# The expert stage of a gated cross-attention block written out tile by tile, with other distances between its steps

## What is computed

```python
# _L1_ffn_ref, x: [16, 256, 256], E = 8 experts, K = 2 per token, HID = 512
probs = jax.nn.softmax(logits, axis=-1)
_, top_k_idx = jax.lax.top_k(logits, K)
...
gate0 = jnp.einsum('bld,ehd->bleh', x, gating_w[:, 0])
gate1 = jnp.einsum('bld,ehd->bleh', x, gating_w[:, 1])
act = jax.nn.gelu(gate0) * gate1
out = jnp.einsum('bleh,ehd,ble->bld', act, linear_w, combine)
...
x = x + jnp.tanh(g_ffn[1]) * _L1_ffn_ref(_layernorm(x, axis=-1), ...)
```

## Time and profile before

| | us |
|---|---|
| median of 3 runs | 1779.32 (1778.08 to 1781.38) |
| the profiled execution | 1782.04 |
| its span, first to last instruction | 1780.2 |
| PE busy | 1522.6 (86%) |
| DVE busy | 1202.0 (68%) |
| ACT busy | 925.8 (52%) |
| POOL busy | 592.0 (33%) |

### The profile page before, as it was taken

The page is one execution under the profiler, slowest core; times in us unless marked ns, Lnnn a source line. Parts: engine busy times, 40 slices in busy tenths (PEclk is TensorE's granted clock), DMA queues, the critical chain, the costliest instruction groups (busy, mean ns, idle before and its releaser), DMA issues. The chain is left out here.

```text
span 1780.2 us, 36819 instructions
## 1 busy us (share of the span) xinstructions
PE 1522.6 (86%) x12540; PEld 1084.8 (61%) x12541; DVE 1202.0 (68%) x3316; ACT 925.8 (52%) x2530; POOL 592.0 (33%) x777
## 2 busy tenths in 40 slices
PE   3899999999999999999999999986538887888784
PEld 2667676676766767667676776755425454555452
DVE  5478888788887888878888788886433433333332
ACT  4377676766767667676676766755112222222221
POOL 3002323233332333323333233332423444444442
PEclk9899999999999999999999999998759999999997
DMA  7101202021020210202102021031016222222224
GB/s 241 60 1 61 66 7 72 7 67 65 9 72 7 66 61 12 72 7 67 56 18 72 2 71 49 8 109 63 20 58 177 45 44 44 44 44 44 44 44 121
DMA packets 78142, 97.97 MB, mean 55 GB/s; under 512 B 20576, under 2 KB 61680, under 8 KB 77936
## 3 DMA queue, kind: packets, MB, share of 16 engines
q1 hardware_dynamic: 51152, 77.01, 13.6%
q0 software_dynamic: 15872, 18.95, 6.6%
q10 hardware_dynamic: 10976, 0.13, 0.3%
HBM read 65.02 MB, written 35.23 MB: 56 GB/s over the span
## 5 line engine op out<-in xcount | busy, mean ns | idle before, releaser
L801 ACT ACTIVATE prob<-S,nm 128x256 f32<-128x256 f32 x512 | 235.5, 474 | 81.8 <-issue 41.2
L794 ACT ACTIVATE pTh<-T 128x512 f16<-128x512 f32 x256 | 139.5, 597 | 136.0 <-PE T L975 135.8
L1303 PE MATMUL S<-GL,xgh 128*128 x576 | 173.8, 384 | 10.1 <-issue 8.8
L1494 DVE TENSOR_REDUCE mx<-S 128x2 f32<-128x512 f32 x256 | 163.3, 679 | 21.2 <-PE S L1048 20.7
L645 POOL TENSOR_SCALAR ve_ln<-mv_ln 128x2 f32<-128x2 f32 x64 | 14.7, 229 | 470.6 <-DVE mv_ln L1468 469.7
L1506 DVE SCALAR_TENSOR_TENSOR pTl<-T,pTh 128x512 f16<-128x512 f32 x256 | 164.1, 682 | 6.5 <-ACT pTh L794 6.5
L716 POOL DMA_INDIRECT xg<-x_rows,trow x72 | 70.4, 978 | 230.2 <-DMA acc_rows<-ysb,yid 99.3
L810 ACT ACTIVATE prob<-prob,rden 128x256 f32<-128x256 f32 x256 | 116.5, 504 | 56.5 <-DVE p0n L1515 55.8
L975 PE MATMUL T<-ident,prob 128*128 128x128 f32 x1024 | 142.2, 283 | 1.6 <-DVE prob L1519 1.4
L953 ACT ACTIVATE aH<-T 128x512 f16<-128x512 f32 x72 | 43.0, 597 | 192.0 <-PE T L975 144.4
L970 PE MATMUL W<-cTh,Wkh 128*128 128x256 f16 x512 | 140.3, 274 | 0.0
(11 more groups left out here) (296 smaller groups left out, 4457.3 us busy)
## 6 DMA issues: line engine op xcount, KB each, us to landing
cx<-in_ctx_dram SPq DMA_DIRECT2D x16, 512.0 KB
gst<-in_L_ffn_gating_w_dram SPq DMA_DIRECT2D x16, 512.0 KB
gating_split<-gsp SPq DMA_DIRECT2D x16, 512.0 KB
GL<-gating_split SPq DMA_DIRECT2D x8, 1024.0 KB
stg<-in_L_xattn_Wkv_dram SPq DMA_DIRECT2D x8, 512.0 KB, 13.5
xl<-in_x_dram SPq DMA_DIRECT2D x16, 256.0 KB
lst<-in_L_ffn_linear_w_dram SPq DMA_DIRECT2D x16, 256.0 KB
xres<-in_x_dram SPq DMA_DIRECT2D x16, 256.0 KB
```

The lines of the kernel that those rows point to most:

```text
L794: A(flat(pTh[:, h, :, :]), T[h][:, :], ACT.Copy).then_inc(s_pTh[h], 1)
L801: ins = A(prob[:, h, t, :], S[h][:, t * NTOK:(t + 1) * NTOK], ACT.Exp, bias=nm[:, h, t:t + 1], scale=SM, accum_out=rs[:, h, t:t + 1])
L1303: ins = M(o[:, :], (xgl if n == 2 else xgh)[r % 2][:, k, :], GLflat[:, bass.ds(w, HID)], start=(k == 0 and n == 0), stop=(k == KD - 1 and ...
L1494: ins = V.tensor_reduce(mx[:, h, :], S[h][:, :].rearrange("p (t k) -> p t k", t=TT), AX.X, ALU.max)
```

## The change

The stage is written out tile by tile on every engine, with no loop, and waits compare with constants. It has 71 tiles instead of 72: N_TILES is the largest number of whole tiles that 8192 pairs in eight groups can need. The table rows of all tiles go to one buffer `tab`, eight tiles ahead; gathers run five tiles ahead into six `xg` buffers, `ysb` has six buffers, and the scatter reads the token numbers from `tab`, so `yid` and its copy go. On POOL the gather of tile i + 5 now stands ahead of the wait for the scatters and of the scatter of tile i. PE's slot i is gate 0 of tile i, row transpose of tile i + 1, linear product of tile i - 2, hidden transpose of tile i - 1, gate 1 of tile i. SP waits for five gathers before it loads the last five experts' weights. The arithmetic of a tile is the same.

```diff
@@ -35,7 +35,7 @@
 EXPERT_ROWS = NTOKENS
-N_TILES = NTOKENS * TOPK // P + E
+N_TILES = (NTOKENS * TOPK + E * (P - 1)) // P
 TABLE_COLS = ((E - 1) * EXPERT_ROWS + N_TILES * P + P - 1) // P
 TABLE_ROWS = TABLE_COLS * P
 ALL_ROWS = NTOKENS + P
@@ -153,6 +153,8 @@
 VECTOR_STEPS = 40
 POOL_CHUNKS = (4, 6)
 POOL_STEPS = 18
+XG, YS, TB = 6, 6, 8
+GATHER_AHEAD, TABLE_AHEAD = 5, 8
 def build(nc, x, ctx, lens, g_xattn, g_ffn, Wq, Wkv, null_kv, Wout, ln_scale, ln_bias, w1, b1, w2, b2,
@@ -332,15 +334,14 @@
         early = (2 * KD * INNER + 2 * KC * 2 * INNER) // GL_SIZE
         GLflat = GL[:, :, :].rearrange("p a b -> p (a b)")
-        trow = [sb(f"trow{i}", [P, 2], I32) for i in range(4)]
-        xg = [sb(f"xg{i}", [P, D]) for i in range(4)]
+        tab = sb("tab", [P, N_TILES, 2], I32)
+        xg = [sb(f"xg{i}", [P, D]) for i in range(XG)]
         xgh = [sb(f"xgh{i}", [P, KD, P], FP16) for i in range(2)]
         xgl = [sb(f"xgl{i}", [P, KD, P], FP16) for i in range(2)]
         gel = sb("gel", [P, HID])
         hid = sb("hid", [P, HID])
         aH, aL = sb("aH", [P, HID], FP16), sb("aL", [P, HID], FP16)
-        ysb = [sb(f"ysb{i}", [P, D]) for i in range(4)]
-        yid = [sb(f"yid{i}", [P, 1], I32) for i in range(4)]
+        ysb = [sb(f"ysb{i}", [P, D]) for i in range(YS)]
         def pb(name):
@@ -413,8 +414,8 @@
         s_bcur = sem("boundaries_picked")
         s_end, s_tiles = sem("batches_done"), sem("tile_steps")
         s_we, s_add = sem("expert_weights_in"), sem("rows_added")
-        s_tab = [sem(f"table_in{i}") for i in range(4)]
-        s_xg = [sem(f"rows_in{i}") for i in range(4)]
+        s_tab = [sem(f"table_in{i}") for i in range(TB)]
+        s_xg = [sem(f"rows_in{i}") for i in range(XG)]
         s_xp, s_xgh, s_xgl = sem("rows_T"), sem("rows_T_high"), sem("rows_T_low")
         s_g0, s_g1, s_gel, s_act = sem("gate0"), sem("gate1"), sem("gelu"), sem("hidden")
         s_ap, s_ah, s_al = sem("hidden_T"), sem("hidden_T_high"), sem("hidden_T_low")
@@ -479,18 +480,6 @@
                 eng.wait_ge(s_init, 1)
                 eng.wait_ge(sem, value)
-        def all_tiles(eng, tile):
-
-            tile(0, 0, 0, True, False)
-            tile(1, 0, 1, True, True)
-            with eng.Fori(0, (N_TILES - 4) // 4) as t:
-                for r in range(2, 6):
-                    tile(t * 4 + r, t + r // 4, r, True, True)
-            for i in range(N_TILES - 2, N_TILES):
-                tile(i, i // 4, i % 4, True, True)
-            tile(N_TILES, N_TILES // 4, N_TILES % 4, False, True)
-
-
         @block.sync
         def _(sp):
             for n, (src, _, _) in enumerate(chunks):
@@ -572,7 +561,7 @@
             sp.wait_ge(s_x4o, 16 * (NB + 1))
             for c in range(TT * TOPK):
                 sp.wait_ge(s_scat[c], 16 * NB)
-            for r in range(3):
+            for r in range(GATHER_AHEAD):
                 sp.wait_ge(s_xg[r], 16)
             for e in range(early, E):
                 expert_in(e)
@@ -711,27 +700,22 @@
             wait_apart(pool, s_x4o, 16 * (NB + 1))
             wait_apart(pool, s_x3o, 16 * (NB + 1))
-            def gather(i, quarter, r):
-                wait_apart(pool, s_tab[r], 16 * (quarter + 1))
-                pool.indirect_dma_start(out=xg[r][:, :], out_offset=None, in_=x4_d,
-                                        in_offset=bass.IndirectOffsetOnAxis(ap=trow[r][:, 0:1], axis=0))\
-                    .then_inc(s_xg[r], 16)
-
-            def tile(i, quarter, r, front, back):
-                if isinstance(i, int) and i == 0:
-                    gather(0, 0, 0)
-                    gather(1, 0, 1)
-                wait_apart(pool, s_add, 16 * (i - 1))
-                if front and not (isinstance(i, int) and i + 2 >= N_TILES):
-                    gather(i + 2, quarter + (r % 4 + 2) // 4, (r + 2) % 4)
-                if back:
-                    b = (r - 1) % 4
-                    wait_apart(pool, s_yw, i)
-                    pool.indirect_dma_start(out=acc_d, out_offset=bass.IndirectOffsetOnAxis(ap=yid[b][:, :], axis=0),
-                                            in_=ysb[b][:, :], in_offset=None, compute_op=ALU.add)\
-                        .then_inc(s_add, 16)
-
-            all_tiles(pool, tile)
+            def gather(i):
+                pool.wait_ge(s_tab[i % TB], 16 * (i // TB + 1))
+                pool.indirect_dma_start(out=xg[i % XG][:, :], out_offset=None, in_=x4_d,
+                                        in_offset=bass.IndirectOffsetOnAxis(ap=tab[:, i, 0:1], axis=0))\
+                    .then_inc(s_xg[i % XG], 16)
+
+            for i in range(GATHER_AHEAD):
+                gather(i)
+            for i in range(N_TILES):
+                if i + GATHER_AHEAD < N_TILES:
+                    gather(i + GATHER_AHEAD)
+                at_least(pool, s_add, 16 * i)
+                pool.wait_ge(s_yw, i + 1)
+                pool.indirect_dma_start(out=acc_d, out_offset=bass.IndirectOffsetOnAxis(ap=tab[:, i, 0:1], axis=0),
+                                        in_=ysb[i % YS][:, :], in_offset=None, compute_op=ALU.add)\
+                    .then_inc(s_add, 16)
         @block.scalar
@@ -930,35 +914,30 @@
             for c in range(TT * TOPK):
                 act.wait_ge(s_scat[c], 16 * NB)
-            def table_in(i, r):
-                at = act.value_load(row0[0:1, pick1(i)], min_val=0, max_val=TABLE_ROWS - P)
-                act.dma_start(trow[r][:, :], table_d[bass.ds(at, P), :]).then_inc(s_tab[r], 16)
-
-            def x_high(i, r):
+            def table_in(i):
+                at = act.value_load(row0[0:1, i:i + 1], min_val=0, max_val=TABLE_ROWS - P)
+                act.dma_start(tab[:, i, :], table_d[bass.ds(at, P), :]).then_inc(s_tab[i % TB], 16)
+
+            def x_high(i):
                 act.wait_ge(s_xp, i + 1)
-                A(xgh[r % 2][:, :, :].rearrange("p a b -> p (a b)"), XP[:, 0:D], ACT.Copy).then_inc(s_xgh, 1)
-
...
+                A(xgh[i % 2][:, :, :].rearrange("p a b -> p (a b)"), XP[:, 0:D], ACT.Copy).then_inc(s_xgh, 1)
+
+            for i in range(TABLE_AHEAD):
+                table_in(i)
+            x_high(0)
+            for i in range(N_TILES + 1):
+                if i < N_TILES:
+                    act.wait_ge(s_g0, i + 1)
+                    at_least(act, s_act, i)
+                    A(gel[:, :], G0[:, :], ACT.Gelu_apprx_tanh, scale=1 / WS).then_inc(s_gel, 1)
+                if i + 1 < N_TILES:
+                    x_high(i + 1)
+                if i >= 1:
                     act.wait_ge(s_ap, i)
                     at_least(act, s_lin, i - 1)
                     A(aH[:, :], AP_[:, :], ACT.Copy).then_inc(s_ah, 1)
-                if front:
-                    act.wait_ge(s_g0, i + 1)
...
+                if i + TABLE_AHEAD < N_TILES:
+                    table_in(i + TABLE_AHEAD)
         @block.tensor
@@ -1289,71 +1268,60 @@
             pe.wait_ge(s_end, 1)
-            def x_T(i, quarter, r):
-                pe.wait_ge(s_xg[r], 16 * (quarter + 1))
+            def x_T(i):
+                pe.wait_ge(s_xg[i % XG], 16 * (i // XG + 1))
                 at_least(pe, s_xgl, i)
                 for k in range(KD):
-                    ins = tr(XP[:, k * P:(k + 1) * P], xg[r][:, k * P:(k + 1) * P])
+                    ins = tr(XP[:, k * P:(k + 1) * P], xg[i % XG][:, k * P:(k + 1) * P])
                 ins.then_inc(s_xp, 1)
-            def gate_half(i, r, g, off, o):
+            def gate_half(i, g, off, o):
                 for k in range(KD):
                     for n in range(3):
                         w = off + ((g * 2 + (n == 1)) * KD + k) * HID
-                        ins = M(o[:, :], (xgl if n == 2 else xgh)[r % 2][:, k, :],
+                        ins = M(o[:, :], (xgl if n == 2 else xgh)[i % 2][:, k, :],
                                 GLflat[:, bass.ds(w, HID)], start=(k == 0 and n == 0), stop=(k == KD - 1 and n == 2))
                 return ins
             def expert(i):
-                return pe.value_load(etile[0:1, pick1(i)], min_val=0, max_val=E - 1)
+                return pe.value_load(etile[0:1, i:i + 1], min_val=0, max_val=E - 1)
             def hidden_T(i):
-                pe.wait_ge(s_act, i)
-                at_least(pe, s_al, i - 1)
+                pe.wait_ge(s_act, i + 1)
+                at_least(pe, s_al, i)
                 for c in range(4):
                     ins = tr(AP_[:, c * P:(c + 1) * P], hid[:, c * P:(c + 1) * P])
                 ins.then_inc(s_ap, 1)
-            ahead = {}
-
...
+            def linear(i, e):
+                pe.wait_ge(s_al, i + 1)
+                at_least(pe, s_yw, i)
+                for c in range(4):
+                    for n in range(3):
+                        w = e * GL_SIZE + G_SIZE + ((c // 2) * 2 + (n == 1)) * 2 * D + (c % 2) * D
+                        ins = M(Y[:, 0:D], (aL if n == 2 else aH)[:, c * P:(c + 1) * P],
```

(49 more changed lines are left out.)

49 lines of the change are left out of this document (removed).

## The result

The changed kernel takes 1679.15 us in the median (1676.95 to 1681.68, four runs), the kernel before 1780.35 us on the same chip (1778.08 to 1781.57). The ratio is 0.9437, with a 95% interval from 0.9419 to 0.9454: 101 us less, where 1682 us was predicted. The profiled execution took 1678.45 us, with a span of 1676.7 us.

A forecast was written before the change was run, and what follows sets the result against it. POOL's scatter-gather ring was taken as the bound, 5.90 us a tile, falling to 4.51. With start delay, load stretch and 66 such steps the gain was 97.5 us: 1779.3 - 97.5 = 1681.8, say 1682 us, range 1675 to 1715.

The forecast's parts named there:

- A ring on POOL bounds the kernel before: Expert stage: scatter, landing, wake, gather, scatter on POOL set the tile at 5.90 us, with PE following.
- The gather leaves the ring: On POOL, the gather now runs under the scatter's landing, so 1.28 us from gather to scatter drops out.
- The first rival: On POOL, a gather behind a scatter slows its landing: ring 5.49 us, time 1747; chance 0.21, spread from 1690 to 1747.
- The ring is then 4.51 us: POOL's scatter distance after the change, from the last four scatters of before: 3.8 us landing plus 0.7 wake.
- The lower bound for the ring, 4.3: POOL's steady tiles: little to be had below 4.51 us, since the shortest steady landing is 3.6 us.
- What is late next is PE, by a hair.: End of the expert stage: PE would allow the last scatter 1.1 us before the scatter ring lets it.
- The ring's side of the sum: POOL: fifth scatter at 1365.7 us, then 66 steps of 4.51, so the last scatter starts at 1663.4.
- PE's side of the sum, 1662.3: PE: first gate 1328.5 us, 71 slots of 4.62, drain 5.5; the last scatter could start at 1662.3.
- the 4.4 to 4.7 that was to show the ring: Sign in the steady stretch: the forecast is wrong if scatters stand over 4.7 or under 4.4 us apart.
- The range's lower end, 1675: Forecast's low end in us, if scatters in the load stretch take 4.8 us each instead of 6.4.
- Slot of 4.62: PE's time for one tile's 30 matmuls without a gap, 4.62 us, taken from the kernel before.
- Table loads +1.6 us: ACT issues eight table loads before its first copy instead of three, delaying the first gate by 1.6 us.

The follow-up runs named there:

- the last experiment: Changed kernel with scatters adding straight into the output, bound's register made once, and the first copy behind the sixth table load instead of the eighth: 1664.56 us, ratio 0.9331.
- the last two: Changed kernel with scatters adding straight into the output and the bound's register made once, without and with the first copy moved sooner: 1668.00 and 1664.56 us.

## Why the prediction was right, point by point

- *A ring on POOL bounds the kernel before.* Right, for the steady tiles. Cutting PE's products there gains 6 us; shortening the ring gains 39 (loop written out) or 65 (gather moved). In step i the gather there waits for every scatter issued so far, up to that of tile i - 2, and so for the last one's landing.
- *The gather leaves the ring; a gather behind a scatter does not slow its landing.* Right. The landing is 3.8 us in the median, as before, now with a gather behind each scatter. The first rival's 5.49 us did not occur. By the Trainium skill, "DMA: Bandwidth & Descriptors", section "Queues, rings and completion order", an increment has to wait for the earlier writes of its DMA engine, and a gather issued later is not among them; the trace agrees.
- *The ring is then 4.51 us (3.8 landing, 0.7 wake).* Mis-sized: 4.08 in the queued stretch, 4.11 in the median of the run without low products. The landing was right; the wake is 0.27 us where the landing decides, not 0.7. The 4.51 came from the last four scatters of before, and they do not show the ring. They stand outside the loop and wait in the same form as in the changed kernel, the scatter itself for the landing and an instruction in front for `ysb`. Two of their three steps were ended by `ysb`, from which they started 0.78 and 0.74 us later, although the profile names the landing for the first; the trace names it for the second:

```profile
1756.36 1.55 POOL L730 DMA_INDIRECT acc_rows<-ysb,yid  x1 [2.96 <-DVE ysb L1808]
```

  The third had a landing of 4.26 us and started 0.27 us behind it. So 4.51 was mostly PE's pace at the end of the stage, and that it fits 3.8 + 0.7 is chance; 0.73 is the wake in the loop. The lower bound for the ring, 4.3, excluded the true value. That the loop's wake would go was not in the sum: the ring fell for two causes, 5.90 to 5.36 by the waits and 5.36 to 4.1 by the gather, where I had one.
- *"What is late next is PE, by a hair."* The order of the two was wrong. PE's slot is 4.56 us and bounds all 60 steady tiles; the ring has 0.45 us of slack in each. The ring's side of the sum said 1663.4, and the last scatter started at 1657.58: these 5.8 us are nearly the whole miss in the profiled execution (span 1676.7, predicted 1682.7).
- *PE's side of the sum, 1662.3.* Its own terms give 1662.0. With the measured start and slot it gives 1328.3 + 71 x 4.56 + 5.5 = 1657.6, right to 0.1 us, and this is luck. PE's last gate product ended at 1650.1, 2.0 us before the sum has it, and the last `ysb` was there at 1655.75:

```profile
1655.27 0.48 DVE L1768 TENSOR_SCALAR ysb<-O,tab 128x256 f32<-128x256 f32 x1 [1.68 <-PE O L1302]
```

  From there PE alone would have let the scatter start 0.78 us later, at 1656.5. It had to wait for the landing of the scatter before. So PE bounds the stage but for its last 1.1 us, which are the ring's.
- *The time, 1682 for 1679.15.* It came closer than the span, because the forecast was taken 2.7 below the profiled execution, as in the kernel before, while the runs after lie 0.7 above theirs. That is luck, and so is the measured distance of the scatters, 4.56, inside the 4.4 to 4.7 that was to show the ring: it is PE's slot, near a ring period of 4.51 that was read from rows in which `ysb` decided.
- *The range's lower end, 1675.* It came from a faster load stretch on the ring's side alone, while the same text put PE's floor at 1681. The measured 1679.15 lies between them, since the slot was shorter than 4.62.
- *Slot of 4.62.* It was read in the old order, where the linear part follows its operands closely. With the linear product two slots behind it is 0.06 to 0.17 us shorter (4.73 with it one slot behind, in the experiment). I had booked nothing for this part of the change; with the rest of the order it is worth about 10 us, since PE is the bound.
- *Table loads +1.6 us, first copy at 1327.5, first gate at 1328.5, first scatter at 1340.1.* Measured 1327.20, 1328.30 and 1339.65.
- *Load stretch, 6.4 us a scatter, fifth at 1365.7.* It started at 1362.82; the landings there were 4.7 in the median, not 5.7, and the wake was shorter. Hidden either way.
- *PE waits a few us for rows near tiles 8 to 10.* It did not in the changed kernel, and by little: with one tile less of lead it waits 4.2 us there, with a start 2.4 us sooner (the last experiment) 2.3 us.
- *What follows the last landing, 15.5 us, is unchanged.* 1676.7 - 1661.27 = 15.4.
- *PE's gaps in every slot; the lock of VectorE.* Neither shows. The scatters' own time is 1583 ns in the median with DVE busy half the time beside them, so the blocking of GpSimd by VectorE in a two-port mode (the Trainium skill, "SBUF — State Buffer", section "Who interferes with whom") did not bear on these DVE operations, as in the trace before.
- *Slower than before.* No run of this structure was, but for the lead of three tiles, whose ring through PE, DVE and POOL was none of my rivals.

## What to carry to other kernels

Ask of each ring which instruction holds the wait: on an instruction in front of a DMA it cost 0.5 us more a tile than on the DMA itself, and only the step from the landing to the next start shows it. Before a period is read from a row of like instructions, see for each step which wait ended last: three steps of 4.51 us here were two waits for `ysb` and one slow landing. When two limits come out within 3% of each other, price both with their own errors: which of them bounds decides what every later edit is worth, here nothing or 0.17 us x 71 for an order on PE.

## What the runs showed of the hardware that was not expected

- The time from the event waited for to the start of the scatter depends on which instruction holds the wait. In the changed kernel the scatter holds the wait for the landing, and a wait of its own in front of it (L715) that for `ysb`. Where the landing came last, a scatter started 0.27 us after it (median of 22); where `ysb` decided, 0.78 us after that (median of 47). With the register move in front holding the wait for the landing it was 0.82 us (median of 70). The two runs with additions straight into the output differ in that move alone and by 19 us. In the steady stretch of the changed kernel `ysb` mostly decides and the 0.78 us cost nothing, since PE bounds.
- A few scatters start late though both that they wait for are there. In the changed kernel one starts at 1509.56, with `issue` as what its idle time is put down to; the landing had come 1.62 us before and its `ysb` 1.66 us before, where 0.27 and 0.78 are the rule:

```profile
1509.56 1.58 POOL L716 DMA_INDIRECT acc_rows<-ysb,tab  x1 [2.48 <-issue]
```

  The changed kernel has three such starts, late by 0.77, 0.88 and 0.29 us. They belong to a place in the program: this one is the 38th scatter, and the 38th starts 1.66 to 1.69 us behind its `ysb` in five other versions too (linear product one slot behind, four gathers ahead, 72 tiles, and the last two). Two landings of 4.9 and 5.2 us stand in the steady stretch, with no weight load in flight. The cause of neither was tried. PE's bound covers them, since about 0.45 us of slack a tile makes one good in two or three tiles.
- A kernel with the same instructions and two gathers less of lead was 14% slower than the changed one (1921.36 against 1679.15): a lead that is one tile too short does not cost a tile's wait, it closes a ring.
